# The first pass of an attention layer: the diagonal block is scored stripe by stripe, and the keys behind a stripe get the mask alone

## The chip, the cores and the metric

The kernel runs on one core of one Trainium2 chip. The core has five engines that run side by side, each with its own list of instructions, and they wait for one another by semaphores. In the profile they are PE (TensorE, the matmul array; PEld is its weight load), DVE (VectorE), ACT (ScalarE), POOL (GpSimd) and SP (SyncE, which issues most DMAs). The metric is the device time of one execution in microseconds (us).

## The reference

Two attention layers and two feed-forward layers stand one behind the other. Only the first attention layer bears on this change: 2 sequences of 2048 tokens, 256 channels, 16 heads of 16 channels, causal, with a distance term.

```python
q, k, v = (proj(q_w), proj(k_w), proj(v_w))
scores = jnp.einsum('bhid,bhjd->bhij', q, k) / scale
scores = scores + alibi[None]                      # -|i - j| * slope of the head
causal = pos[None, :] <= pos[:, None]
scores = jnp.where(causal[None, None], scores, -jnp.inf)
attn = jax.nn.softmax(scores, axis=-1)
out = jnp.einsum('bhij,bhjd->bhid', attn, v)
```

## The kernel before, in words

The work of this layer is cut into 8 units (2 sequences by 4 groups of 4 heads, `UNITS`), and each unit into 4 query tiles of 512 queries (`qt`). Each unit goes through the scores twice.

The first pass finds the largest score of each query. Queries lie on the partitions, 128 at a time (block `r` of the tile), keys along the columns. One step is a `Chunk`: it fills one of two slots of PSUM (two banks each, 1024 columns) with the scores of two heads by 512 keys, or, at the diagonal (`c == qt`), of four heads by 128 keys (r = 0), four by 256 (r = 1), or twice two by 384 (r = 2) and by 512 (r = 3). DVE takes the maximum of each row (L1512, `part_max`), and that frees the slot. When a tile is done, DVE takes `neg_max`, POOL splits it into three bf16 parts, PE turns them (`SendMaxima`, L989), DVE copies them out and SP sends them into the rows that the second pass multiplies with.

PE fills a chunk in stripes. The array of 128 columns is used as four tiles of 32 columns, one for each stripe of 32 queries; four matmuls (L976), one for each stripe, run in it side by side. At the diagonal four more (L982) follow for each head: an identity times the mask, accumulated onto the last 128 key columns, which puts -1e30 on the keys behind each query.

The second pass (`Score`, L1003) makes the scores again with keys on the partitions, ACT takes their exponentials (L1334), POOL clears the part above the diagonal (L1878), and PE multiplies them with the values (`Weigh`, L1025, fp32, which is two rounds of four matmuls for each key block). At the end of a tile ACT copies the sums out and PE turns them (`Divide`, L1035).

The order of all these steps on every engine is settled before the program is built, by a planner (`FrontPlan`): it keeps an estimated clock for PE, DVE, ACT and POOL, adds a price to them for each step, and takes the next step among those that are ready by its clocks. The price of a chunk on PE is 0.42 ns for each column and, at the diagonal, 46 ns for each head. So a changed price can change the order of everything behind it. Behind the first layer (from about 960 us) the order is another planner's, which the change does not touch.

Of the kernel before, what the change touches and what calls it, by code (L numbers as in the profile page):

```python
# [14 lines left out]
P = 128  # L15
# [4 lines left out]
TILE = 512  # L20
# [108 lines left out]
STRIPE = 32  # L129
# [3 lines left out]
class FrontPlan:  # L133
# [165 lines left out]
    def chunk(self):  # L299
        u, qt, r, heads, c, width, per_bank, last = self.chunks[self.n_chunk]  # L300
        self.n_chunk += 1
        n, room = self.take_ring()
        self.steps.append(Chunk(u, qt, r, heads, c, width, per_bank, n, room))
        columns = len(heads) * width
        self.pe += columns * 0.42 + 46 * len(heads) * (c == qt)
        self.dve = max(self.dve, self.pe + self.PE_LAG) + columns / 0.96 + 75
        self.free[room.slot] = self.dve + self.LAG
        self.max_columns += columns
        if last:
            t = u * QT + qt  # L310
            self.steps.append(Maxima(u, qt, t, n, self.turned_ring.get(t - 2, -1) + 1))
            self.dve += 200
            self.pool = max(self.pool, self.dve + self.LAG) + 1150
            self.to_send.append((u, qt, t, self.pool + self.LAG))
# [580 lines left out]
def tensor_front(nc, m, s, plan):  # L895
    pe = nc.tensor
    for step in plan.steps:
# [25 lines left out]
        elif isinstance(step, Values):  # L923
            if step.tile == 0:
                pe.wait_ge(s.w0_in[2], 16)
            wait_room(pe, s, step.room)
            for half, b in enumerate(MAX_BANKS[step.room.slot]):
                for j in range(2):
                    o = (half * 2 + j) * P
                    for c in range(KC):  # L930
                        mm = pe.matmul(m.bank[b][:, j * D:(j + 1) * D], m.x_t[step.tile % 2][:, c, o:o + P],
                                       m.w_qkv0[2][:, c, :], start=(c == 0), stop=(c == KC - 1))
                mm.then_inc(s.v_projected, 1)

        elif isinstance(step, FoldFirst):
            f = m.folding
            pe.wait_ge(s.spec_in, 80)
            wait_room(pe, s, step.room)
            for terms, b in zip(((("wr", "cos"), ("wi", "sin")), (("wi", "cos"), ("wr", "nsin"))), MAX_BANKS[step.room.slot]):
                for half in range(KC):  # L940
                    for i, (l, r) in enumerate(terms):
                        for c in range(KC):
                            mm = pe.matmul(m.bank[b][:, half * D:(half + 1) * D], f[l][:, c, half * P:(half + 1) * P],
                                           f[r][:, c, :], start=(i == 0 and c == 0), stop=(i == 1 and c == KC - 1))
            mm.then_inc(s.ring_filled, 1)

        elif isinstance(step, FoldSecond):
            f = m.folding
            wait_room(pe, s, step.room)
            pe.wait_ge(s.ring_taken, step.first + 1)  # L950
            for half in range(KC):
                for i, (l, r) in enumerate((("art", "cos"), ("ait", "nsin"))):
                    for c in range(KC):
                        mm = pe.matmul(m.bank[MAX_BANKS[step.room.slot][0]][:, half * D:(half + 1) * D],
                                       f[l][:, c, half * P:(half + 1) * P], f[r][:, c, :],
                                       start=(i == 0 and c == 0), stop=(i == 1 and c == KC - 1))
            mm.then_inc(s.ring_filled, 1)

        elif isinstance(step, Chunk):
            slot = step.u % 3  # L960
            if step.r == 0 and step.heads[0] == 0 and step.c == 0:
                if step.u == 0:
                    pe.wait_ge(s.first_in[step.qt], 16 * (2 * len(TERMS) + (1 + GH if step.qt == 0 else 0)))
                elif step.qt == 0:
                    pe.wait_ge(s.op_in[slot], operand_bytes(step.u))
            if step.ring == 0:
                pe.wait_ge(s.masks_in, 16)
                pe.wait_ge(s.identb_in, 16)
            wait_room(pe, s, step.room)
            w = step.width  # L970
            for n, h in enumerate(step.heads):
                bank = m.bank[MAX_BANKS[step.room.slot][n // step.per_bank]]
                o = n % step.per_bank * w

                for q in range(0, P, STRIPE):
                    mm = pe.matmul(bank[q:q + STRIPE, o:o + w],  # L976
                                   m.q_op[slot][:, step.qt, h, step.r * P + q:step.r * P + q + STRIPE],
                                   m.k_op[slot][:, h, step.c * TILE:step.c * TILE + w], start=True, stop=True,
                                   skip_group_check=True)
                if step.c == step.qt:  # L980
                    for q in range(0, P, STRIPE):
                        mm = pe.matmul(bank[q:q + STRIPE, o + w - P:o + w], m.ident_b[:, q:q + STRIPE], m.masks[:, 1, :],  # L982
                                       start=False, stop=True, skip_group_check=True)
            mm.then_inc(s.ring_filled, 1)

        elif isinstance(step, SendMaxima):
            pe.wait_ge(s.max_split, 4 * (step.t + 1))
            wait_room(pe, s, step.room)
            pe.transpose(m.bank[MAX_BANKS[step.room.slot][0]].bitcast(BF16)[0:3 * MAXIMA, 0:P],  # L989
                         m.max_parts[step.t % 2][:, :, :].rearrange("p a n -> p (a n)"),  # L990
                         m.ident_b[:, :]).then_inc(s.ring_filled, 1)

        elif isinstance(step, Score):
            slot, t, w = step.u % 3, step.u * QT + step.qt, TILE - step.q0
            if step.first:
                pe.wait_ge(s.max_rows[t % 2], 48 * (t // 2 + 1))
            if step.ring_clear:
                pe.wait_ge(s.ring_taken, step.ring_clear)
            if step.before:
                pe.wait_ge(s.exped, step.before)  # L1000
            for n, h in enumerate(step.heads):
                for k in range(0, P, STRIPE):
                    mm = pe.matmul(m.bank[step.bank][k:k + STRIPE, n * w:(n + 1) * w],  # L1003
                                   m.k_op[slot][:, h, step.kb * P + k:step.kb * P + k + STRIPE],
                                   m.q_op[slot][:, step.qt, h, step.q0:TILE], start=True, stop=True,
                                   skip_group_check=True)
            mm.then_inc(s.scored, 1)

        elif isinstance(step, Weigh):
            b, g = UNITS[step.u]  # L1010
            if step.first:
                if step.t:
                    pe.wait_ge(s.sums_taken, step.t)
                else:
                    pe.wait_ge(s.sums_cleared, 1)
            tile = b * TPB + step.blocks[0][0] // BPT
            if g == 0 and step.blocks[0][0] % BPT == 0 and step.blocks[0][0] // BPT == step.qt:
                pe.wait_ge(s.v_by_act, tile + 1)
                pe.wait_ge(s.v_by_dve, tile + 1)
            pe.wait_ge(s.exped, step.scored)  # L1020
            if step.selected:
                pe.wait_ge(s.selected, step.selected)
            for n, (kb, q0, at, place) in enumerate(step.blocks):
                for h in range(GH):
                    mm = pe.matmul(m.sums[32 * h:32 * h + HD + 1, q0:TILE], m.v_aug[:, b * BPB + kb, g * GH + h, :],  # L1025
                                   m.p_ring[:, place, h, at:at + TILE - q0], start=(step.first and n == 0),
                                   stop=(step.last and n == len(step.blocks) - 1), skip_group_check=True)
            mm.then_inc(s.weighed, 1)

        elif isinstance(step, Divide):  # L1030
            a = step.t % 2
            pe.wait_ge(s.sums_taken, step.t + 1)
            wait_room(pe, s, step.room)
            for r in range(BPT):
                mm = pe.transpose(m.bank[MAX_BANKS[step.room.slot][0]][:, r * P:(r + 1) * P], m.acc_t[a][:, r * P:(r + 1) * P],  # L1035
                                  m.ident[:, :])
            mm.then_inc(s.ring_filled, 1)
# [1195 lines left out]
```

## Time and profile before

| | us |
|---|---|
| median of 3 runs | 1549.0 |
| lowest and highest | 1548.0, 1552.71 |
| the profiled execution | 1549.12 |
| its span, first to last instruction | 1547.1 |
| PE busy, DVE busy, ACT busy | 1417.8, 1076.7, 854.5 |

The profiled execution and the median are 0.1 us apart, so a difference worked out from the trace can be set against either. Matmuls overlap in the trace: of four that run side by side each is shown with its full length. So the lengths are no cost; what four matmuls cost is read from one row's start to the next row's start.

### The profile page before, as it was taken

What the parts mean: (1) busy time and instruction counts of PE and PEld (TensorE: products, weight loads), DVE (VectorE), ACT (ScalarE), POOL (GpSimd) and SP (SyncE); (2) the same over time, 40 slices, a digit from 0 to 9 for tenths busy, and PEclk for the clock granted to TensorE, in tenths of its full rate; (3) what the DMA queues carried; (4) which work ended last, traced back from release to release, by engine and by line L of the source; (5) the groups of instructions that cost most, each with busy time, mean ns of one, the idle gap of its engine ahead of it and who ended that gap; (6) DMA issues with size and microseconds to landing.
All of it is one profiled execution on the core that took longest, in us unless ns stands there. A gap on an engine that the chain in (4) does not pass through costs nothing. (4 is left out here: it accounts for less than half of the span.)

```text
span 1547.1 us, 43841 instructions
## 1 busy us (share of the span) xinstructions
PE 1417.8 (92%) x18356; PEld 858.0 (55%) x18356; DVE 1076.7 (70%) x1993; ACT 854.5 (55%) x1783; POOL 240.9 (16%) x380
## 2 busy tenths in 40 slices
PE   7878999999999999999999999898977559999998
PEld 4434444444444444444444453786754259999997
DVE  2376768888887888878888871554558647677675
ACT  2335647767677677676776767552425323433333
POOL 3212021011101111021111110000112611111111
PEclk9999999999999999999999999897998779999999
DMA  8574018513215113142300000570032254554541
GB/s 234 158 120 91 22 64 120 66 26 49 34 28 68 27 30 47 28 59 28 88 3 3 4 2 2 190 257 7 1 98 79 76 208 171 182 186 178 186 175 71
DMA packets 77823, 134.09 MB, mean 87 GB/s; under 512 B 12226, under 2 KB 64443, under 8 KB 72252
## 3 DMA queue, kind: packets, MB, share of 16 engines
q1 hardware_dynamic: 72412, 121.45, 30.4%
q0 software_dynamic: 3408, 8.43, 1.6%
q8 instruction: 146, 2.39, 0.7%
q10 hardware_dynamic: 1808, 1.41, 0.3%
q14 instruction: 49, 0.40, 0.1%
HBM read 67.77 MB, written 23.11 MB: 59 GB/s over the span
## 5 line engine op out<-in xcount | busy, mean ns | idle before, releaser
L1512 DVE TENSOR_REDUCE part_max<-pair 128x2 f32<-128x1024 f32 (+2 forms) x576 | 647.5, 1162 | 115.3 <-PE pair L982 57.4
L1334 ACT ACTIVATE big<-pair 128x512 f32<-128x512 f32 (+1 forms) x1120 | 565.2, 610 | 239.7 <-PE pair L1003 237.4
L976 PE MATMUL pair<-big 128*32 128x512 bf16 (+3 forms) x5120 | 359.6, 352 | 29.1 <-DVE part_max L1512 24.2
L1003 PE MATMUL pair<-big 128*32 128x512 bf16 (+3 forms) x5120 | 345.1, 351 | 3.4 <-issue 1.4
L1025 PE MATMUL pair<-big 128*17 128x512 f32 (+3 forms) x2560 | 280.3, 528 | 2.7 <-issue 2.3
L976 PEld LDWEIGHTS pair<-big 128*32 128x32 bf16 x5120 | 135.1, 97 | 198.4 <-DVE part_max L1512 98.8
L1003 PEld LDWEIGHTS pair<-big 128*32 128x32 bf16 x5120 | 126.8, 96 | 174.3 <-ACT big L1334 88.7
L1347 ACT ACTIVATE std<-moments,eps_col 128x1 f32<-128x1 f32 (+1 forms) x110 | 32.5, 295 | 261.6 <-DVE moments L1550 261.6
L1878 POOL TENSOR_SCALAR_AFFINE_SELECT big<-big 128x512 f32<-128x512 f32 x128 | 80.0, 637 | 474.3 <-ACT big L1334 474.3
L1242 PEld LDWEIGHTS pair<-big,tok 128*128 128x128 f32 x1248 | 147.8, 195 | 4.9 <-DVE big L1778 3.0
L1242 PE MATMUL pair<-big,tok 128*128 128x128 f32 x1248 | 148.3, 278 | 2.4 <-DMA tok<-big 1.4
L1254 PE MATMUL pair<-big 128*128 x624 | 141.0, 379 | 0.0
L1254 PEld LDWEIGHTS pair<-big 128*128 128x128 f32 x624 | 115.6, 190 | 14.1
L982 PE MATMUL pair<-masks,ident_b 128*32 128x128 bf16 x2048 | 102.0, 223 | 0.0
L1025 PEld LDWEIGHTS pair<-big 128*17 128x17 f32 x2560 | 70.1, 96 | 50.2 <-issue 25.9
L1915 POOL DMA_INDIRECT out<-big x39 | 38.4, 985 | 263.8 <-DVE big L1819 263.8
L919 PE MATMUL pair<-big 128*128 128x512 f32 x128 | 65.4, 658 | 5.9 <-DVE big L1476 5.1
L982 PEld LDWEIGHTS pair<-masks,ident_b 128*32 128x32 bf16 x2048 | 56.5, 99 | 25.8 <-issue 21.4
L1481 DVE SCALAR_TENSOR_TENSOR big<-pair,big 128x512 f32<-128x512 f32 x32 | 22.1, 692 | 58.3 <-ACT big L1317 58.3
L1080 PE MATMUL pair<-big 128*128 128x256 f32 x256 | 58.8, 383 | 0.0
L1443 ACT ACTIVATE big<-pair,columns 128x128 f32<-128x128 f32 x156 | 44.4, 365 | 18.7 <-PE pair L1242 12.3
L1778 DVE TENSOR_SCALAR big<-pair,columns 128x128 f32<-128x128 f32 x78 | 28.5, 405 | 36.5 <-PE pair L1230 24.0
(163 smaller groups left out, 1279.0 us busy)
## 6 DMA issues: line engine op xcount, KB each, us to landing
tok<-big SPq DMA_DIRECT2D x39, 1024.0 KB
big<-in_L_ffn_w SPq DMA_DIRECT2D x16, 1024.0 KB, 12.3
big<-split_dram SPq DMA_DIRECT2D x216, 64.0 KB, 4.6
split_dram<-big SPq DMA_DIRECT2D x32, 384.0 KB, 2.7
big<-split_dram SPq DMA_DIRECT2D x42, 256.0 KB, 6.1
big<-routed_dram SPq DMA_DIRECT2D x39, 129.0 KB, 2.1
tok<-in_L_attn_x SPq DMA_DIRECT2D x8, 512.0 KB, 9.2
big<-in_c_query_rows SPq DMA_DIRECT2D x8, 512.0 KB, 5.3
```

Of the source, the lines that this page charges most:

```text
L919: mm = pe.matmul(m.bank[b], m.w_qkv0[side][:, c, step.m * P:(step.m + 1) * P], m.x_t[step.tile % 2][:, c, :], start=(c == 0), stop=(c == K ...
L976: mm = pe.matmul(bank[q:q + STRIPE, o:o + w], m.q_op[slot][:, step.qt, h, step.r * P + q:step.r * P + q + STRIPE], m.k_op[slot][:, h, step ...
L982: mm = pe.matmul(bank[q:q + STRIPE, o + w - P:o + w], m.ident_b[:, q:q + STRIPE], m.masks[:, 1, :], start=False, stop=True, skip_group_che ...
L1003: mm = pe.matmul(m.bank[step.bank][k:k + STRIPE, n * w:(n + 1) * w], m.k_op[slot][:, h, step.kb * P + k:step.kb * P + k + STRIPE], m.q_op[ ...
L1025: mm = pe.matmul(m.sums[32 * h:32 * h + HD + 1, q0:TILE], m.v_aug[:, b * BPB + kb, g * GH + h, :], m.p_ring[:, place, h, at:at + TILE - q0 ...
L1080: mm = pe.matmul(m.bank[b][:, j * D:(j + 1) * D], m.turned_x[slot][:, c, r * P:(r + 1) * P], weight[:, c, :], start=(c == 0), stop=(c == K ...
L1242: mm = pe.matmul(m.bank[b][:, j * P:(j + 1) * P], w1[:, c, f * P:(f + 1) * P], m.xln_t[i % 2][:, c, :], start=(c == 0), stop=(c == KC - 1))
L1254: mm = pe.matmul(m.bank[b][:, 0:D], m.hidden_t[i % 2][:, f, :], m.w2[:, bass.ds(e, 1), f, :].rearrange("p a n -> p (a n)"), start=(f == 0) ...
L1334: act.activation(m.p_ring[:, step.place, step.heads[0]:step.heads[-1] + 1, step.at:step.at + w], m.bank[step.bank][:, 0:len(step.heads) * ...
L1443: done = act.activation(m.hidden_t[i % 2][:, j, :], m.bank[b][:, j * P:(j + 1) * P], ACTF.Relu, bias=col[:, j, bass.ds(e, 1)])
L1512: dve.tensor_reduce(m.part_max[(step.u * QT + step.qt) % 2][:, step.r, step.heads[0]:step.heads[0] + n, step.c], banks[:, :, 0:w], X, ALU. ...
L1878: pool.affine_select(weights, weights, pattern=[[0, GH], [1, P]], compare_op=ALU.is_ge, fill=zero, base=0, channel_multiplier=-1).then_inc ...
```

## The change

It touches the diagonal chunks of the first pass with more than 128 keys (r = 1, 2, 3). A stripe that begins at query q of its block now scores only the keys up to its own 32 (`keys`), so for a width of 512 the four stripes get 416, 448, 480 and 512 columns where each had 512. Then four matmuls put the mask on each stripe's own 32 keys, and three more (stripes 2, 1 and 0, in this order) write the mask alone over the 32, 64 and 96 columns behind. The chunk with r = 0 stays as it was. DVE still reads all columns. In the planner the price of a trimmed head at the diagonal falls from 46 to 12 ns.

```diff
-        self.pe += columns * 0.42 + 46 * len(heads) * (c == qt)
+        self.pe += columns * 0.42 + (46 if width == P else 12) * len(heads) * (c == qt)
...
+                diagonal, trimmed = step.c == step.qt, step.c == step.qt and w > P
                 for q in range(0, P, STRIPE):
-                    mm = pe.matmul(bank[q:q + STRIPE, o:o + w],
+                    keys = w - P + q + STRIPE if trimmed else w
+                    mm = pe.matmul(bank[q:q + STRIPE, o:o + keys],
                                    m.q_op[slot][:, step.qt, h, step.r * P + q:step.r * P + q + STRIPE],
-                                   m.k_op[slot][:, h, step.c * TILE:step.c * TILE + w], start=True, stop=True,
+                                   m.k_op[slot][:, h, step.c * TILE:step.c * TILE + keys], start=True, stop=not diagonal,
                                    skip_group_check=True)
-                if step.c == step.qt:
+                if trimmed:
+
+                    for q in range(0, P, STRIPE):
+                        own = o + w - P + q
+                        mm = pe.matmul(bank[q:q + STRIPE, own:own + STRIPE], m.ident_b[:, q:q + STRIPE],
+                                       m.masks[:, 1, q:q + STRIPE], start=False, stop=True, skip_group_check=True)
+                    for q in reversed(range(0, P - STRIPE, STRIPE)):
+                        mm = pe.matmul(bank[q:q + STRIPE, o + w - P + q + STRIPE:o + w], m.ident_b[:, q:q + STRIPE],
+                                       m.masks[:, 1, q + STRIPE:P], start=True, stop=True, skip_group_check=True)
+                elif diagonal:
```

The first place is one head of a chunk with r = 2 on PE. Before, with the matmul of the second pass that follows (`x4` is the four stripes; L976 scores, L982 masks, L1003 the second pass):

```order
L976 MATMUL pair<-big 32x384 x4
L982 MATMUL pair<-masks,ident_b 32x128 x4
L976 MATMUL pair<-big 32x384 x4
L982 MATMUL pair<-masks,ident_b 32x128 x4
L1003 MATMUL pair<-big 32x512 x4
```

And one such head now (L978 scores, L986 the own keys' mask, L989 the mask alone):

```order
L978 MATMUL pair<-big 32x288
L978 MATMUL pair<-big 32x320
L978 MATMUL pair<-big 32x352
L978 MATMUL pair<-big 32x384
L986 MATMUL pair<-masks,ident_b 32x32 x4
L989 MATMUL pair<-masks,ident_b 32x32
L989 MATMUL pair<-masks,ident_b 32x64
L989 MATMUL pair<-masks,ident_b 32x96
```

Eight matmuls became eleven. The fourth stripe keeps its full 384 columns and has no fill; the first has the shortest score and the longest fill.

The second place is the start of a unit on PE, at the chunks of its first tile (qt = 0), all of them at the diagonal. Before, from the end of the chunk with r = 0 (L1025 are weighs of the unit before: 17x512 is a whole key block, 17x384, 17x256 and 17x128 are key blocks at the diagonal):

```order
988 L982 MATMUL pair3<-masks,ident_b 32x128 x4
989 L1025 MATMUL pair1<-big 17x256 x4
990 L1025 MATMUL pair1<-big 17x128 x4
991 L976 MATMUL pair2<-big 32x256 x4
992 L982 MATMUL pair2<-masks,ident_b 32x128 x4
993 L976 MATMUL pair2<-big 32x256 x4
```

The same place now, where the chunk with r = 0 ends:

```order
1230 L993 MATMUL pair3<-masks,ident_b 32x128 x4
1231 L1036 MATMUL pair1<-big 17x512 x4
1232 L978 MATMUL pair2<-big 32x160
1233 L978 MATMUL pair2<-big 32x192
1234 L978 MATMUL pair2<-big 32x224
1235 L978 MATMUL pair2<-big 32x256
```

Further on in the same run, before, from the end of the chunk with r = 1 to the second chunk with r = 2 (L989 is SendMaxima of the unit before):

```order
998 L982 MATMUL pair2<-masks,ident_b 32x128 x4
999 L976 MATMUL pair3<-big 32x384 x4
1000 L982 MATMUL pair3<-masks,ident_b 32x128 x4
1001 L976 MATMUL pair3<-big 32x384 x4
1002 L982 MATMUL pair3<-masks,ident_b 32x128 x4
1003 L989 MATMUL pair2<-ident_b,max_parts1 48x128
1004 L976 MATMUL pair3<-big 32x384 x4
```

And now, at its two ends (L1000 is SendMaxima, L1036 a weigh). Ahead of the first chunk with r = 2:

```order
1263 L989 MATMUL pair2<-masks,ident_b 32x96
1264 L1036 MATMUL pair1<-big 17x384 x4
1265 L978 MATMUL pair3<-big 32x288
1266 L978 MATMUL pair3<-big 32x320
1267 L978 MATMUL pair3<-big 32x352
```

Between the first and the second:

```order
1280 L989 MATMUL pair3<-masks,ident_b 32x96
1281 L1036 MATMUL pair1<-big 17x256 x4
1282 L1000 MATMUL pair2<-ident_b,max_parts1 48x128
1283 L1036 MATMUL pair1<-big 17x128 x4
1284 L978 MATMUL pair3<-big 32x288
```

Before, two weighs (17x256, 17x128) stood between the chunks r = 0 and r = 1 and none further on; the whole block and the 17x384 one had been issued ahead of r = 0. Now four weighs stand in the run, each between two chunks. This is so at the start of 6 of the 8 units (2 to 7); in units 0 and 1 the place reads as before.

## Rows read from the trace of the kernel before

**Rows 1.** The page, part 1: busy us, share of the span, instructions.

```profile
PE 1417.8 (92%) x18356; PEld 858.0 (55%) x18356; DVE 1076.7 (70%) x1993; ACT 854.5 (55%) x1783; POOL 240.9 (16%) x380
```

**Rows 2.** Windows, 300 to 900 us: columns named in the first row.

```profile
core 0: us, PE busy (x) PEld busy (x) DVE busy (x) ACT busy (x) POOL busy (x), PEclk, DMA share, GB/s
300.00:900.00 600.00, 582.30 (x11160) 265.84 (x11156) 505.10 (x525) 432.50 (x858) 79.98 (x192) 1.00 0.21 34
```

**Rows 3.** Waits of PE, 300 to 900 us: total us, times, longest.

```profile
PE pair L976 <- DVE part_max L1512: 8.7, 18, 0.6
PE pair L989 <- DVE part_max L1512: 4.3, 6, 0.7
```

**Rows 4.** Timeline of PE, one chunk with r = 2: start, length, matmuls.

```profile
506.43 0.34 PE L976 MATMUL pair<-big 128*32 128x384 bf16 x4
506.60 0.23 PE L982 MATMUL pair<-masks,ident_b 128*32 128x128 bf16 x4
506.65 0.34 PE L976 MATMUL pair<-big 128*32 128x384 bf16 x4
```

**Rows 5.** Timeline, 503.8 to 505.5 us: PE and its weight loads.

```profile
503.61 0.39 PE L1003 MATMUL pair<-big 128*32 128x512 bf16 x4
503.83 0.60 PE L976 MATMUL pair<-big 128*32 128x512 bf16 x8
...
504.27 0.10 PEld L1003 LDWEIGHTS pair<-big 128*32 128x32 bf16 x4 [0.33 <-ACT big L1334]
504.27 0.40 PE L1003 MATMUL pair<-big 128*32 128x512 bf16 x4
...
504.50 1.03 PE L1025 MATMUL pair<-big 128*17 128x512 f32 x8
...
505.35 0.39 PE L976 MATMUL pair<-big 128*32 128x512 bf16 x4
```

**Rows 6.** Timeline at 1177 us: the narrowest matmuls behind each other.

```profile
1177.36 0.22 PE L1202 MATMUL pair<-acc_t 128*128 128x24 bf16 x3
...
1177.43 0.18 PE L1204 MATMUL pair<-acc_t 128*128 128x32 bf16 x1
```

**Rows 7.** Timeline of PE, the run at the start of unit 4.

```profile
519.07 0.23 PE L976 MATMUL pair<-big 128*32 128x128 bf16 x4
519.12 0.23 PE L982 MATMUL pair<-masks,ident_b 128*32 128x128 bf16 x4
519.18 0.82 PE L1025 MATMUL pair<-big 128*17 128x256 f32 x16
519.83 0.28 PE L976 MATMUL pair<-big 128*32 128x256 bf16 x4
...
520.43 0.23 PE L982 MATMUL pair<-masks,ident_b 128*32 128x128 bf16 x4
520.90 0.35 PE L976 MATMUL pair<-big 128*32 128x384 bf16 x4 [0.23 <-DVE part_max L1512]
...
521.29 0.23 PE L982 MATMUL pair<-masks,ident_b 128*32 128x128 bf16 x4
522.12 0.22 PE L989 MATMUL pair<-ident_b,max_parts 128*48 128x128 bf16 x1 [0.60 <-DVE part_max L1512]
522.89 0.35 PE L976 MATMUL pair<-big 128*32 128x384 bf16 x4 [0.56 <-DVE part_max L1512]
...
523.82 0.23 PE L982 MATMUL pair<-masks,ident_b 128*32 128x128 bf16 x4
524.58 0.40 PE L976 MATMUL pair<-big 128*32 128x512 bf16 x4 [0.52 <-DVE part_max L1512]
...
525.07 0.23 PE L982 MATMUL pair<-masks,ident_b 128*32 128x128 bf16 x4
525.71 0.61 PE L976 MATMUL pair<-big 128*32 128x512 bf16 x8 [0.41 <-DVE part_max L1512]
```

**Rows 8.** Timeline of DVE, the same run.

```profile
520.15 2.69 DVE L1512 TENSOR_REDUCE part_max<-pair 128x4 f32<-128x512 f32 x3 [0.21 <-DVE neg_max L1519]
522.75 0.21 DVE L1528 COPY max_t<-pair 48x128 bf16<-48x128 bf16 x1
523.56 3.22 DVE L1512 TENSOR_REDUCE part_max<-pair 128x2 f32<-128x768 f32 x3 [0.60 <-PE pair L982]
```

## The prediction

> **What bounds the kernel now.** I read the page's first part, then the windows of the first layer, then the waits of PE, and then the timeline of single steps. The page gives PE 92% of the span [rows 1]. The change lies in the first layer, which ends near 960 us, and there the share is higher: from 300 to 900 us PE is busy 582 of 600 us, DVE 505, ACT 433, and the clock is granted in full, 2.4 GHz [rows 2]. The reader is to see that DVE, with 84%, is no far second. What is left of waiting in PE is on DVE only, and it has a pattern: in those 600 us 18 waits at chunks and 6 at SendMaxima [rows 3], three and one for each of the six unit starts (units 2 to 7) that lie there. The timeline shows where. At the start of unit 4 the six chunks of the first tile follow each other with nothing between that PE could do instead; DVE needs longer for each (six reduces, 2.69 and 3.22 us for three each, almost without a gap [rows 8]) than PE does, and PE stands still between them [rows 7]. Everywhere else one column group follows the next without a hole. So PE's column time is the bound, but for one stretch of about 5 us in each unit, where it is DVE.
>
> **What one trimmed head costs.** Before: for a width of 384, from the scores' start to the masks' 0.17 us and from there to the next head 0.05 us, 0.22 us together [rows 4]. 384 columns at 2.4 GHz are 160 ns, 128 are 53 ns, and 2 to 3 ns lie over each group; so a head costs w/2.4 + 58 ns, of which the masks are 56. The four stripes of a group start within some 10 ns: a group's length is that much more than a single matmul's.
>
> After, the stripes have unequal widths, and no row of this trace shows such a group: in every one the four are equal. So I bound it from both sides. The columns for stripe 0 are (w - 96) + 32 + 96, for stripe 3 w + 32, for the two between the same w + 32. If each stripe runs on by itself, a head costs w/2.4 + 20 ns: 38 ns less. If matmuls start in the order in which they are issued, it is otherwise. Stripe 3's own mask can start only when its full score is through, w/2.4 + 2 + 10 ns after the head began, and the fills stand behind it in the list. The last of them is stripe 0's 96 columns: it starts 2 to 6 ns later, runs 42 ns, and only then can the next head's stripe 0 start. That is w/2.4 + 61 ns, 3 ns more than before. The columns saved are spent waiting for stripe 3.
>
> A weight load can add to this, since stripe 2's own mask begins only some 18 ns before stripe 3's, and the load for its fill can't go before it. What a late load costs: at 504.27 the L1003 group got its weights only as it started, and the next one came 0.23 us later in place of 0.216, so about 13 ns [rows 5]; that stays hidden. The narrowest matmuls in the trace, 24, 16, 8 and 32 columns, each with a load of 128 columns, follow each other every 24 ns (four starts from 1177.36 to 1177.43) [rows 6]. If that holds between mask and fill of one stripe, the fills start 7 ns later and a head costs 10 ns more than before. I take in-order starts and the late load of rows 5, since those are loads of the same 32 columns: +3 ns for a head, with -38 and +10 as ends, and a far one below.
>
> On the order of starts the Trainium skill has two rules that differ. "TensorE: Matmul & The Clock Gate", Part 3, "The mechanism", says that matmuls begin and end strictly in program order and that only weight loads are pulled ahead; by it the saving is gone. "TensorEngine Tiling (Array Packing)", "Key Properties", says that tiles work independently; by it the 38 ns are saved. With equal widths both give what the rows show, so the trace does not decide, and I keep them as forecast and rival. The first page also has a floor of about 25 ns between starts; the trace agrees (24 ns).
>
> **How many heads count.** A unit has 48 trimmed heads, 12 for each tile. The 12 of its first tile are in the stretch that DVE bounds, where 3 ns or 38 make no difference. That leaves 36 in 8 units, 288: 288 x 3 ns = +0.9 us (ends -10.9 and +2.9).
>
> **What the new order moves.** This is the larger term. The lower price makes PE look earlier to the planner, and so, at six unit starts, weighs that were issued ahead of the run now stand inside it. A whole block's weigh takes 0.85 us (504.50 to 505.35) [rows 5], so one of 384 columns 0.64, of 256 0.43, of 128 0.21; the last two are the 0.65 us from 519.18 to 519.83 [rows 7]. PE's holes in the run, each from the end of the last masks (their start and 0.055 us) to the next row: 0.41, 0.78, 0.77 less the 0.06 of the turn, 0.70 and 0.58, about 3.2 us [rows 7]. Now the 0.64 us weigh fills the first, the 0.43 the second, the 0.21 the third: 1.28 us of work that PE had to do anyway and that now costs nothing while it fits. The first does not quite fit (0.64 against 0.41), and the weigh between r = 0 and r = 1 grows from 0.65 to 0.85; together DVE gets its next chunk 0.2 to 0.4 us later, of which the reduce still running hides some. So 1.0 us a unit at least. At most it is what the run holds in addition, 2.13 us for 0.65, or 1.5 us. I take 1.2, for six units -7.2 us (ends -6 and -9; -0 if the run merely grows).
>
> No other queue is moved past. Operands' DMAs are issued by the same rule, ACT and DVE have the same instructions, and 13 double weighs split into single ones, which costs no columns. SendMaxima comes behind one weigh more, yet it already waited 0.6 us for its slot. Cover gone: the second pass of the next tile needs the last weigh of the tile before, which moves some 1 to 2 us later; Divide, which needs it too, comes only behind the whole run, so it is not late next.
>
> **Sum.** 1549.1 + 0.9 - 7.2 = 1542.8; with the floor of rows 6 half believed, 1543.5. The forecast is 1543.5 us, its own range 1540 to 1547.
>
> **Rivals.** Stripes run by themselves: the 38 ns are saved on 288 heads, -10.9 us, or 28 ns (-8.1) if the 24 ns hold between mask and fill. With the order, 1549.1 - 9.5 - 7.2 = 1532.4. For it: the four tiles have weights and outputs of their own. Against it: starts are never seen out of order, though they had no cause to be.
>
> Narrow groups can't hide their loads (slower): the shortest distance of two four-stripe groups that the trace has is 55 ns, at 128 columns (519.07 to 519.12) [rows 7]. If it is also the least that a reload of the same stripe allows, then own masks and fills cost 56 ns each where the one mask group cost 56: +56 ns a head, +16.0 us. It decides as soon as the start of L986 to the start of L989 on the same stripe is above some 45 ns, where it outweighs the order's gain. 1549.1 + 16.0 - 7.2 = 1557.9. Against it: 24 ns with wider loads in rows 6.
>
> The order brings nothing: the new places of the weighs make DVE wait for its chunks as long as PE waited before, because DVE, 84% busy, is nearly the bound around the run too. Then only the heads are left, 1550 to 1552. The planner's belief that PE saves 34 ns a head, where it saves none, speaks for it: it hands out steps earlier than their inputs are ready.
>
> **How the numbers follow.** Chances: forecast 0.47, stripes by themselves 0.27, loads not hidden 0.12, order without gain 0.14. A difference under 0.3%, 4.6 us, can't be told from none. Faster is the second case whole and of the forecast's own range what lies under 1544.4, about two thirds: 0.60. Slower is the third case and little of the fourth: 0.15. The same: 0.25. The range reaches down to the middle of the second case, 1532, and up past the fourth to 1554; outside are that case's lower part and the third, together under 0.2.
>
> **What would show it.** In a warm chunk with r = 2 the distance from one head's first score to the next head's: 0.22 us by the forecast, 0.18 if stripes run alone, 0.27 if loads aren't hidden; and the start of stripe 0's own mask, before or after stripe 3's score has run. At the unit starts: the waits of PE on `part_max` down by about 1.2 us each, DVE's gaps in the run not grown by as much. From one unit start to the next, SendMaxima to SendMaxima, it should be some 1 us less than before. The prediction is wrong if the second layer's part moves, or if new waits on ACT's exponentials appear in front of weighs.

## The result and the profile after

The changed kernel takes 1565.27 us (median of 4 runs, 1562.32 to 1572.22), the kernel before 1548.5 us: a ratio of 1.0109, 95% interval 1.0069 to 1.015. It is slower by 17 us, where 1543.5 was forecast and 1554 was the upper end. The profiled execution took 1562.32 us, 13.2 more than that of before. Its spread is wider: 10 us in four runs, 5 before.

The head of the page, and its queue for instructions. What answers to [rows 1]:

```profile
span 1560.3 us, 46151 instructions
PE 1416.9 (91%) x19508; PEld 871.3 (56%) x19508; DVE 1075.3 (69%) x1993; ACT 852.9 (55%) x1783; POOL 240.7 (15%) x380
...
q8 instruction: 155, 2.54, 0.7%
```

The same queue in the kernel before:

```profile
q8 instruction: 146, 2.39, 0.7%
```

PE has 1152 matmuls and 1152 weight loads more. Instructions come into the core as data do, over a DMA queue, 16 KB a packet (2.54 MB in 155). That q8 is PE's queue, with 256 instructions to a packet, follows from the counts: 2304 more instructions of PE brought 9 more packets.

The heads first. The timeline of PE at a chunk with r = 2, which answers to [rows 4]:

```profile
514.52 0.34 PE L978 MATMUL pair<-big 128*32 128x288 bf16 x4
514.64 0.20 PE L986 MATMUL pair<-masks,ident_b 128*32 128x32 bf16 x2
514.67 0.20 PE L989 MATMUL pair<-masks,ident_b 128*32 128x96 bf16 x1
514.68 0.18 PE L986 MATMUL pair<-masks,ident_b 128*32 128x32 bf16 x1
514.69 0.19 PE L989 MATMUL pair<-masks,ident_b 128*32 128x64 bf16 x1
514.69 0.18 PE L986 MATMUL pair<-masks,ident_b 128*32 128x32 bf16 x1
514.71 0.18 PE L989 MATMUL pair<-masks,ident_b 128*32 128x32 bf16 x1
514.71 0.33 PE L978 MATMUL pair<-big 128*32 128x288 bf16 x4
```

From one head to the next it is 0.19 us, where it was 0.22. And the matmuls do not start in the order of the list: the first stripe's fill of 96 columns, last in the list, starts at 514.67, ahead of two stripes' own masks. Stripe by stripe the array runs on by itself. The 96-column fill begins 0.03 us after its stripe's own mask (28 ns in the trace), which is near the 24 ns of [rows 6] and above the 16 ns that the columns would allow. There is a risk in this that the change does not deal with: the semaphore that lets DVE read the chunk is raised by the last matmul in the list, which is this fill. At the second head of this chunk it starts at 514.86 us, and four matmuls that stand before it in the list start after it, by up to 0.04 us. No run here shows whether DVE ever read too early.

Now the waits. Waits of PE from 300 to 900 us, the view of [rows 3] (total us, times, longest):

```profile
PE pair L978 <- DVE part_max L1523: 6.1, 12, 0.6
PE pair L978 <- issue: 4.7, 3, 2.9
PE pair L989 <- issue: 3.5, 2, 2.1
PE pair L1046 <- issue: 3.5, 1, 3.5
PE pair L1014 <- DMA big<-max_t: 2.3, 5, 0.6
```

The waits on DVE at the unit starts have fallen from 13.0 to 6.1 us, as forecast: the weighs fill them. What has grown is "issue", time in which PE waits for nothing that the profile shows: 11.7 us here, in six places. It was there before as well. The same view of the kernel before has two more rows than [rows 3] shows:

```profile
PE pair L1025 <- issue: 2.3, 1, 2.3
PE pair L1003 <- issue: 1.4, 1, 1.4
```

Over the whole first layer (60 to 945 us) issue is now 18.7 us, and was 3.7. The longest but one is that at 607 us. The timeline of PE there:

```profile
605.64 0.59 PE L1014 MATMUL pair<-big 128*32 128x512 bf16 x5
606.03 0.64 PE L978 MATMUL pair<-big 128*32 128x512 bf16 x8
606.46 1.06 PE L1036 MATMUL pair<-big 128*17 128x512 f32 x8
611.01 1.01 PE L1046 MATMUL pair<-ident,acc_t 128*128 128x128 f32 x4 [3.49 <-issue]
```

And the windows around it (us, PE, PEld, DVE, ACT, POOL busy, granted clock, DMA share, GB/s):

```profile
596.00:602.00 6.00, 6.00 (x139) 2.91 (x135) 5.64 (x6) 4.62 (x11) 2.54 (x4) 1.00 1.12 123
602.00:606.50 4.50, 4.50 (x121) 2.79 (x117) 3.29 (x4) 3.04 (x7) 0.00 (x0) 1.00 1.11 113
606.50:611.00 4.50, 1.02 (x12) 0.24 (x5) 1.71 (x2) 1.21 (x3) 0.00 (x0) 0.95 0.36 37
611.00:614.00 3.00, 2.99 (x24) 1.37 (x27) 0.78 (x3) 1.09 (x2) 0.00 (x0) 0.51 0.02 5
```

For ten microseconds the 16 DMA engines have been full (share 1.1) with the operands of a later unit. PE meanwhile used up its instructions: 260 matmuls and 252 loads in 10.5 us are two packets' worth. Then it stands for 3.5 us, and DVE and ACT run dry behind it. After it the clock is granted at half, 1.2 GHz (0.51), for the next 3 us, a second price on top of the hole. The trace has two instruction packets in this burst, one that starts at 597.97 us and one at 607.96; outside bursts they follow each other every 4 to 9 us.

The second of them has landed at 609.63 us, and PE starts again 1.4 us later. This is so everywhere. The fourteen profiles of this document have 32 issue waits of more than 1 us in the first layer. In each, PE starts again 1.2 to 1.8 us after a packet of q8 has landed, and that packet had started 7.8 to 11.1 us after the one before it. So what PE stands for there is its next packet of instructions.

### The profile page after: what moved, and what is told of

It is laid out like the page before. It is cut to its first block and busy times, and to the rows that moved or that the text cites. A ratio compares the mean times of both kernels' runs of the same rounds, so it can differ in the third digit from the quotient of the medians.

```text
span 1560.3 us, 46151 instructions
## 1 busy us (share of the span) xinstructions
PE 1416.9 (91%) x19508; PEld 871.3 (56%) x19508; DVE 1075.3 (69%) x1993; ACT 852.9 (55%) x1783; POOL 240.7 (15%) x380
## 3 DMA queue, kind: packets, MB, share of 16 engines
q8 instruction: 155, 2.54, 0.7%
## 5 line engine op out<-in xcount | busy, mean ns | idle before, releaser
L978 PE MATMUL pair<-big 128*32 128x512 bf16 (+9 forms) x5120 | 362.1, 348 | 36.1 <-DVE part_max L1523 21.4
L1014 PE MATMUL pair<-big 128*32 128x512 bf16 (+3 forms) x5120 | 354.3, 353 | 6.7 <-issue 3.0
L1036 PE MATMUL pair<-big 128*17 128x512 f32 (+3 forms) x2560 | 288.5, 533 | 0.7 <-POOL big L1889 0.3
L978 PEld LDWEIGHTS pair<-big 128*32 128x32 bf16 x5120 | 147.2, 97 | 181.9 <-DVE part_max L1523 82.7
L1014 PEld LDWEIGHTS pair<-big 128*32 128x32 bf16 x5120 | 127.1, 95 | 171.5 <-ACT big L1345 90.1
L1036 PEld LDWEIGHTS pair<-big 128*17 128x17 f32 x2560 | 72.3, 97 | 46.2 <-issue 22.3
L989 PE MATMUL pair<-masks,ident_b 128*32 128x96 bf16 (+2 forms) x1152 | 77.6, 191 | 3.5 <-issue 3.5
L986 PE MATMUL pair<-masks,ident_b 128*32 128x32 bf16 x1536 | 80.1, 180 | 0.0
L919 PE MATMUL pair<-big 128*128 128x512 f32 x128 | 62.2, 631 | 6.2 <-DVE big L1487 5.4
L989 PEld LDWEIGHTS pair<-masks,ident_b 128*32 128x32 bf16 x1152 | 55.6, 98 | 11.8 <-issue 3.1
L986 PEld LDWEIGHTS pair<-masks,ident_b 128*32 128x32 bf16 x1536 | 45.8, 96 | 22.3 <-issue 16.3
```

The lines of the kernel that those rows point to most:

```text
L919: mm = pe.matmul(m.bank[b], m.w_qkv0[side][:, c, step.m * P:(step.m + 1) * P], m.x_t[step.tile % 2][:, c, :], start=(c == 0), stop=(c == K ...
L978: mm = pe.matmul(bank[q:q + STRIPE, o:o + keys], m.q_op[slot][:, step.qt, h, step.r * P + q:step.r * P + q + STRIPE], m.k_op[slot][:, h, s ...
L986: mm = pe.matmul(bank[q:q + STRIPE, own:own + STRIPE], m.ident_b[:, q:q + STRIPE], m.masks[:, 1, q:q + STRIPE], start=False, stop=True, sk ...
L989: mm = pe.matmul(bank[q:q + STRIPE, o + w - P + q + STRIPE:o + w], m.ident_b[:, q:q + STRIPE], m.masks[:, 1, q + STRIPE:P], start=True, st ...
```

## The experiments

The kernels ran in three groups (e1 to e4; a1 and e5 to e7; the t's and e8). Those of a group ran on one chip and share the runs of the kernel before; each ratio is against those. Runs of different groups are compared by their ratios. The pair of theories is: the supply of PE's instructions (theory 1), and the new order as such (theory 2).

**e1_more_matmuls.** The order and the columns of before, but eleven matmuls a head.

```diff
-                    for q in range(0, P, STRIPE):
+                    whole = range(0, P, STRIPE) if w == P else (P - STRIPE,)
+                    for half in (range(2) if w > P else ()):
+                        for q in range(0, P - STRIPE, STRIPE):
+                            k = half * P // 2
+                            mm = pe.matmul(bank[q:q + STRIPE, o + w - P + k:o + w - P // 2 + k], m.ident_b[:, q:q + STRIPE],
+                                           m.masks[:, 1, k:k + P // 2], start=False, stop=True, skip_group_check=True)
+                    for q in whole:
```

> The kernel before, in its own order, but the mask of stripes 0, 1 and 2 of the trimmed heads goes in as two matmuls of 64 columns in place of one of 128: eleven matmuls a head as in the changed kernel, the same columns as before. Theory 1 (supply of instructions: PE's own instructions arrive late while operands are loaded, and 1152 more matmuls with as many weight loads make that worse): 5 to 15 us slower than before, PE waits put down to issue rise from 3.7 us to 10 us or more. Theory 2 (the new order is what costs): within 2 us of before, since columns and order are the same.

Measured: 1557.82 us against 1550.75, 1.0045 (1.0027 to 1.0063), 7 us slower. Issue waits 9.2 us in the first layer, 3.7 before. Theory 1 expected this, and theory 2 can't explain it.

**e2_old_price.** The changed matmuls in the order of before; the edit is against the changed kernel.

```diff
-        self.pe += columns * 0.42 + (46 if width == P else 12) * len(heads) * (c == qt)
+        self.pe += columns * 0.42 + 46 * len(heads) * (c == qt)
```

> The changed kernel's matmuls with the planner's old price of 46 ns, so in the order of before. Theory 1 (supply of instructions): heads save 27 ns each on 288 heads, 8 us, and the stalls of 15 us stay, so 3 to 10 us slower than before. Theory 2 (order): the stalls go with the order, and 8 us faster than before.

Measured: 1550.64 us, 1.0003 (0.9987 to 1.0019): no difference. This fell between the two: neither 3 us slower nor 8 faster. The profiled execution has only 4.5 us of issue waits. So the many matmuls alone do not make 17 us. That e1's +7 and the trimmed columns' gain cancel is a reading of the two results; the profile of e2 has far less waiting for issue than that of e1 (4.5 us against 9.2), and more on `max_t` (4.8 against 2.3).

**e3_new_order.** The matmuls of before with the new price.

```diff
-        self.pe += columns * 0.42 + 46 * len(heads) * (c == qt)
+        self.pe += columns * 0.42 + (46 if width == P else 12) * len(heads) * (c == qt)
```

> The kernel before with the planner's new price of 12 ns: the order of the changed kernel with the matmuls of before. Theory 1 (supply of instructions): 0 to 4 us faster than before, since the weighs fill the holes at the unit starts and the number of instructions is the old one. Theory 2 (order): 10 to 20 us slower than before.

Measured: 1554.06 us, 1.0026 (1.0009 to 1.0044), 4 us slower, with 7.5 us of issue waits in a profiled execution that was one of its fastest. The order costs something, where theory 1 had expected nothing or a gain, but a quarter of what theory 2 needs.

**e4_one_mask.** Trimmed scores, and one mask matmul for each stripe, from its own 32 keys to the end of the block: eight matmuls a head, order of before (the edit is shown against the changed kernel; the price is the old one). It rests on this: a stripe's score, with start=True, makes the later matmul without it add on the columns that the score wrote and overwrite the columns behind.

```diff
                 if trimmed:
                     for q in range(0, P, STRIPE):
                         own = o + w - P + q
-                        mm = pe.matmul(bank[q:q + STRIPE, own:own + STRIPE], m.ident_b[:, q:q + STRIPE],
-                                       m.masks[:, 1, q:q + STRIPE], start=False, stop=True, skip_group_check=True)
-                    for q in reversed(range(0, P - STRIPE, STRIPE)):
-                        mm = pe.matmul(bank[q:q + STRIPE, o + w - P + q + STRIPE:o + w], m.ident_b[:, q:q + STRIPE],
-                                       m.masks[:, 1, q + STRIPE:P], start=True, stop=True, skip_group_check=True)
+                        mm = pe.matmul(bank[q:q + STRIPE, own:o + w], m.ident_b[:, q:q + STRIPE],
+                                       m.masks[:, 1, q:P], start=False, stop=True, skip_group_check=True)
```

> Order of before (price 46). Scores are trimmed as in the changed kernel, but the mask of a stripe is one matmul that starts at its own 32 keys and runs to the end of the block (128, 96, 64, 32 columns): eight matmuls a head as before. Theory 1 (supply of instructions): no stalls beyond those of before, heads at w/2.4 + 18 ns in place of + 58, up to 40 ns on 288 heads: 7 to 12 us faster than before. Theory 2 (order): the same, so this run does not part them; it tells what stripes running by themselves are worth. If masks of unequal width did not overlap, it would be at 0.

Measured: 1543.81 us, 0.9949 (0.9932 to 0.9967), 7 us faster. The timeline of PE, two heads with r = 2:

```profile
503.92 0.34 PE L978 MATMUL pair<-big 128*32 128x288 bf16 x4
504.05 0.23 PE L985 MATMUL pair<-masks,ident_b 128*32 128x128 bf16 x4
504.10 0.35 PE L978 MATMUL pair<-big 128*32 128x288 bf16 x4
```

0.18 us a head, 0.22 before [rows 4]. The idea of the change is sound; its eleven matmuls are not.

**a1_changed_again.** The changed kernel unaltered, in the second group.

> The changed kernel once more, beside the others of this group. The first four runs were 1562 to 1572 us; both theories expect 12 to 20 us slower than before, with waits put down to issue of 10 us or more. If it came out within 6 us of before, the first four runs were chance.

Measured: 1557.07 us against 1544.56, 1.0098 (1.0064 to 1.0132). The stalls repeat: its six holes over 1 us in the first layer all lie within 3 us of one of the seven in the first profile, and the one near 607 us has the same length, 3.48 us for 3.49. So they belong to the program, not to chance.

**e5_one_mask_new_price.** The matmuls of e4 in the order of the changed kernel.

```diff
-        self.pe += columns * 0.42 + 46 * len(heads) * (c == qt)
+        self.pe += columns * 0.42 + (46 if width == P else 12) * len(heads) * (c == qt)
```

> One mask matmul a stripe (eight matmuls a head, trimmed scores) with the price of 12 ns, so in the order of the changed kernel. It differs from the changed kernel by 1152 matmuls and as many weight loads alone. Theory 1 (supply of instructions makes most of the 17 us): 10 us or more faster than the changed kernel, 0 to 5 us faster than before. Theory 2 (the new order costs by itself, whatever the number of instructions): within 5 us of the changed kernel.

Measured: 1539.08 us, 0.9976 (0.9963 to 0.9988). Of the changed kernel's +0.98% this run keeps nothing, with the same order and the same columns: 18 us lie between the two, and what differs is the 2304 further instructions. (Up to 3.5 us of it is array time, since the separate fill keeps a head at 0.19 us where the single mask has 0.18.) Against e4 the order costs 0.27% again, as between e3 and the kernel before.

**e6_changed_few_loads.** The operands of units 3 to 7 are loaded for one row of sixteen; the rest stays an earlier unit's. All instructions stay.

```diff
...
+        if u >= 3:
+            if qt == QT:
+                sp.dma_start(m.k_op[slot][rows.start:rows.start + 1, :, :],
+                             operand_source(m, u, i, 1, slice(0, LENGTH))[0:1, :, :]).then_inc(s.op_in[slot], 16)
+            else:
+                sp.dma_start(m.q_op[slot][rows.start:rows.start + 1, qt, :, :],
+                             operand_source(m, u, i, 0, slice(qt * TILE, (qt + 1) * TILE))[0:1, :, :]).then_inc(s.op_in[slot], 16)
-        if qt == QT:
+        elif qt == QT:
```

> The changed kernel in which the operands of units 3 to 7 are loaded for one row of sixteen only (the rest stays that of an earlier unit), so the bursts of data transfers beside the first layer's work are nearly gone; number and order of all instructions are kept. Theory 1 (PE's instructions are late because their fetch stands behind those transfers): the waits put down to issue behind 300 us go to below 2 us, and the kernel is 8 to 14 us faster than the changed one. Rival (PE's sequencer is simply too slow for so many instructions, without any transfer): the stalls stay as they are.

Measured: 1534.91 us, 0.9953 (0.9934 to 0.9972): 22 us faster than the changed kernel with its loads, more than expected. Its waits of PE from 300 us to the layer's end:

```profile
PE pair L978 <- DVE part_max L1523: 6.1, 12, 0.6
PE pair L1014 <- DMA big<-max_t: 2.5, 6, 0.6
PE pair L954 <- DVE max_t L1539: 0.6, 1, 0.6
```

Not one wait for issue is left. The number of instructions is the same, so PE's sequencer is fast enough for them; what it lacked was their arrival.

**e7_before_few_loads.** The same edit in the kernel before.

> The kernel before with the same loads left out. Theory 1: its two or three stalls of 1.6 to 2.4 us go, so 3 to 5 us faster than before; and the kernel e6 with the changed matmuls is then 5 to 10 us faster than this one, since heads save 27 ns each on 288 heads and nothing takes it back. Rival (sequencer too slow): this one as before, e6 still slower than it by more than 10 us.

Measured: 1538.11 us, 0.9966 (0.9952 to 0.9979), 5 to 6 us faster; no issue waits. But e6 is only 3 us below it, not 5 to 10.

The time from one unit start to the next (SendMaxima to SendMaxima, us) shows it without any theory:

| unit | 1 | 2 | 3 | 4 | 5 | 6 |
|---|---|---|---|---|---|---|
| before | 101.2 | 100.2 | 102.3 | 100.1 | 102.2 | 99.9 |
| changed | 109.9 | 102.6 | 100.8 | 106.0 | 103.7 | 99.7 |
| before, few loads (e7) | 100.4 | 100.6 | 100.6 | 99.8 | 99.8 | 100.1 |
| changed, few loads (e6) | 104.3 | 98.7 | 98.8 | 98.8 | 98.7 | 98.9 |
| e1's matmuls, few loads (t1) | 102.4 | 99.8 | 100.1 | 99.9 | 100.6 | 100.6 |
| trimmed, old order, few loads (t2) | 105.5 | 99.8 | 99.1 | 99.1 | 99.4 | 100.2 |
| new order, few loads (t3) | 99.6 | 99.6 | 99.4 | 98.9 | 98.9 | 99.6 |

The edit leaves the loads of units 1 and 2 as they are, the last of which run beside unit 1; there e6 still has a stall of 2.5 us. From unit 2 on it needs 98.8 us a unit, where e7 needs 100.2.

**t1_more_matmuls_few_loads, t2_old_price_few_loads, t3_new_order_few_loads.** e1, e2 and e3, each with the edit of e6.

> e1 (eleven matmuls a head with the columns and the order of before) with the operand loads of units 3 to 7 left out but for one row of sixteen. e1 was 0.45% slower than before. If that came from instructions that arrive late behind the transfers, this is within 1.5 us of the kernel before without those loads (e7, 0.34% faster than before). If the eleven matmuls cost in the array or in the sequencer, it stays 5 to 7 us slower than e7.

> e2 (the changed matmuls in the order of before) with the same loads left out. Against e7 it shows what trimmed heads are worth when nothing stalls: 27 ns on 288 heads are 7.8 us, so 1.1% faster in all than before, if PE bounds all heads outside the unit starts. If DVE (84% busy) takes part of it back, 3 to 6 us better than e7.

> e3 (the matmuls of before in the new order) with the same loads left out. With loads the new order cost 0.26%. If it costs because instruction pages fall worse against the bursts of transfers, this is at e7 or up to 4 us faster. If the order itself is worse (new small waits spread over the unit), it is 2 to 5 us slower than e7.

Measured, against the kernel before: t1 0.9995 (0.998 to 1.001), t2 0.9955 (0.9936 to 0.9974), t3 0.9934 (0.9918 to 0.9951); e7 was 0.9966. t1 came out 4 to 5 us above e7, and so missed the 1.5 us. Its waits from 60 to 300 us tell of half of that:

```profile
PE pair L1009 <- issue: 2.2, 1, 2.2
```

That one lies beside the loads that stayed; behind 300 us it has none, and its units 2 to 6 take what e7's take, 100.2 us on average. The rest does not lie in the first layer. In the two profiled executions, which lie 6.7 us apart, t1 is 2.7 us behind e7 at the last SendMaxima, 2.0 of them in unit 1, and the other 4 come behind the layer, where both have the same instructions. t2 is 1.7 us better than e7, with intervals that overlap. Its profiled execution, one of its slowest, gains 0.7 us a unit on e7 from unit 2 on and loses 5.1 in unit 1, where the loads stayed, so that gain and loss nearly cancel. t3 is 5 us better than e7: without the bursts the new order is a gain, with them (e3) it is a loss of 4.

**e8_one_mask_all_blocks.** e4 with the first block of each tile (r = 0) trimmed too.

```diff
-                diagonal, trimmed = step.c == step.qt, step.c == step.qt and w > P
+                diagonal, trimmed = step.c == step.qt, step.c == step.qt
```

> e4 (one mask matmul a stripe, order of before) with the first block of each tile (r = 0, 128 keys) trimmed in the same way: its heads need w/2.4 + 18 ns in place of + 58, on 96 heads outside the unit starts, up to 3.8 us. Loads are the original ones. Expected 8 to 13 us faster than before, if PE bounds there; if the reduces of DVE bound those chunks, no better than e4 (0.5% faster than before).

Measured: 1533.56 us against 1543.99, 0.9942 (0.9923 to 0.9961). It beats both kernels, by 9 us and by some 25. Over e4 (0.9949) it gains nothing that these intervals can tell; in the two profiled executions its first layer is 4.4 us shorter, where up to 3.8 was expected.

## Why the prediction was wrong

**The bound.** Right: the column time of PE, and DVE at the unit starts. Incomplete: PE's own instructions are one more stream, which competes with the operands for the DMA engines, and the profile before already had its traces: 146 packets in q8, and 3.7 us of issue waits between 300 and 900 us. "What is left of waiting in PE is on DVE only" is a wrong reading of the view behind [rows 3], which has two rows on issue between 300 and 900 us as well.

**What one head costs.** Wrong, and in the good direction. I took in-order starts and +3 ns; the rival with stripes that run by themselves was the right one, with its variant of 24 ns between mask and fill: 218 to 192 ns (w = 384), 26 where that variant said 28. On 288 heads this is -7.5 us, where the sum had +0.9. (The forecast's own terms add up to w/2.4 + 56 to 60 ns and not to 61, so its +3 is a little high, by 0.3 us in all.) The Trainium skill's rule in "TensorE: Matmul & The Clock Gate" (Part 3, "The mechanism"), that matmuls begin strictly in program order, does not hold for stripes of unequal width here: the fill at 514.67 starts ahead of two matmuls that stand before it in the list. The Trainium skill's page "TensorEngine Tiling (Array Packing)", "Key Properties", which says that tiles work independently, has it right.

**The order.** The forecast was -7.2 us. Its mechanism was seen (DVE waits 13.0 to 6.1 us), and without the bursts it is worth -5 us (t3 against e7). But with the bursts it turns into +4 (e3; e5 against e4 as well). What is seen to take part of it back are issue waits: 7.5 us in e3 and 3.7 before, 8.6 in e5 and 2.9 in e4. A second cause is likely but not shown. SendMaxima now has 1.92 us of weighs ahead of it in the run (0.85, 0.64 and 0.43), before 0.65, which "it already waited 0.6 us for its slot" did not cover. And the second pass now waits for its rows, 2.3 us on `max_t` in five places where before it was 0.6 in one. But kernels in the old order have such waits too (e1 2.3, e4 2.1, e2 4.8 us), so they can't be put down to the new order.

**The step that failed.** It is the sum, which priced eleven matmuls in place of eight by their columns and put the supply of their instructions at nothing, and the sentence "No other queue is moved past". The queue is that of PE's instructions. More instructions use up a packet sooner; while the operands of a later unit fill all 16 engines, the next packet comes later, up to 11 us after the one before it, and PE stands until it is there. The forecast was 1543.5 us, the result 1565.3: PE's waits for issue went from 3.7 to 18.7 us. Shown: more instructions alone cost 7 us (e1) and the stalls go with the transfers (e6, e7, and t1 behind 300 us). Shown as well: number and order do not simply add up. Extra matmuls cost 18 us in the new order (changed against e5) but 7 in the old one (e2 against e4), up to 3.5 of each being array time. Why the new order meets the bursts worse I can only argue: at 605 us PE does a chunk with r = 1 shortly before it runs dry, 44 matmuls and as many loads in less than 0.6 us, the densest kind of chunk. The cause of that part stays open.

The "Runtime: NRT & Kernel Launch" page of the Trainium skill, section "Instruction fetch mechanics", says that instructions come in blocks of 16 KB over the engine's own DMA queue, which agrees with q8. It also says that the fetch is hidden because the sequencer dispatches more slowly than the fetch fills. The 3.49 us at 607 us contradict that for a stretch in which the DMA engines are full.

**The ledger.** Of the 13.2 us between the two profiled executions, 16.0 lie between the last SendMaxima of unit 0 and that of unit 7 (710.3 us before, 726.3 now). Up to there the changed kernel is 1.3 us quicker, and behind it 1.5 us, so the second layer's part did not grow. In that stretch: issue waits +15.0; waits on DVE -6.7 (14.3 to 7.6); waits on `max_t` +2.3; waits on ACT +0.2; heads -6.6 (252 at 26 ns). That is +4.2. The clock adds to it: PE was granted half clock in six stretches of 3.4 us, and in two before, so 13.7 us more; at half speed this is at most 6.8 us of column time. Four of the six begin within 1.3 us of the end of a hole of 2.1 to 4.0 us. Together that is up to 11; the rest, 5 us or more, is not placed. Part of it is that the issue waits as listed count from the modelled end of a long matmul: the hole at 607 is 3.7 us by the starts, 3.5 as listed.

**The other rivals.** The slower one came nearest (1557.9 against 1565.3), by luck, since its mechanism is not there: a fill follows its own mask after 28 ns, where it needed more than 45. The one in which the order brings nothing has it wrong too: the waits on DVE did fall.

## What to carry to other kernels

Before you split one matmul into several narrow ones, count instructions as well as columns, and look for "issue" waits of PE in the profile before: here they said that the supply of instructions had no slack at that place. See whether they coincide with stretches in which the DMA share is near 1. Where a mask or a fill can be one matmul with start=False over written and unwritten columns, it gives the columns without the instructions.

## What the runs showed of the hardware

- Four column tiles of 32 run independently and start out of program order when their widths differ (514.67 ahead of 514.68 and 514.69). The shortest distance of two starts on one tile in that head was 25 ns, behind a matmul of 32 columns.
- A stall of 3.5 us came from PE's instruction packets being late beside data transfers, at a DMA share of 1.1. PE started again 1.2 to 1.8 us after its packet had landed. Taking the data away took 22 us from the changed kernel and 5 to 6 from the kernel before.
- That stall was followed by 3 us at a granted clock of 0.51; of the seven holes of over 1 us, the four that half clock followed were 2.1 to 4.0 us long, the three others 1.4, 1.5 and 2.5.
- A matmul without start added on columns that its stripe's score had written and overwrote those that it had not (the masks of e4, e5 and e8 rest on it).
